# A fused convolution, mixture and upsampling kernel: a ring of three residual buffers (five at the end), and bilinear upsampling split by axis

## The chip, the cores and the metric

The kernel runs on one core of one Trainium2 chip. The metric is the device time of one execution in microseconds. All inputs and the output lie in device memory; x and the output are 268 MB each.

## The reference

x is a float32 tensor of 8 batches, 512 channels, 128 x 128. What is computed (cut to what matters):

```python
# block 1, with sx = x
x = conv(sx, w_down, stride 2, pad 1, groups=256)        # 2 channels -> 1, 3x3: (8, 256, 64, 64)
labels = kmeans(normalised x[0])                         # 8 clusters of the 256 channels, 10 iterations
v5 = mean of x over the channels of each cluster         # (8, 8, 64, 64)
mu, var = gmm_fit(v5 as 4096 points of 8 numbers)        # 2 components, 10 EM iterations, for each batch
gate = sigmoid(sum over components of ordered mu * w_conv)[:, cluster of the channel]
pre_up = gate * x + x
up = repeat(pre_up, 2, axis=1) * w_up                    # (8, 512, 64, 64)
y = bilinear_up_x2(up) + sx                              # (8, 512, 128, 128)
def bilinear_up_x2(x):
    rows = x[:, :, y0, :] * (1 - fy) + x[:, :, y1, :] * fy
    return rows[:, :, :, x0] * (1 - fx) + rows[:, :, :, x1] * fx
# block 2, on y (weights w_guide, w_fuse, bn_*)
s = clip(w_guide @ mean of y over the image, 0, 6)       # 128 numbers per batch
shift = clip(batchnorm(w_fuse @ s), 0, 6)                # 512 numbers per batch
out = y + shift
```

So for each batch: out = x + shift + scale * (bilinear upsampling of the small convolution result), where scale and shift are numbers per channel that are known only once the whole batch has been convolved and its EM iterations have run. x is therefore read twice: once for the convolution, once as the residual.

## The kernel before

**Tiling.** A batch is 16 steps (`STEPS`): two tiles `t` of 128 small channels, by eight blocks of 16 image rows (`S` = 8, counted by `u` from 0 to 3 and `h` 0 or 1). A step convolves 16 rows of 256 input channels to 8 rows of 64 for 128 channels, and upsamples 8 rows of 64 to 16 rows of 128, each used for the two output channels that share it.

**Stages.** Stage `j` (0 to 9) convolves batch j, runs EM of batch j-1 and writes out batch j-2, step by step side by side. Stage 0 only convolves; then comes the clustering; stage 1 convolves and runs EM; stages 2 to 7 do all three; stage 8 (`B`) does EM and output; stage 9 only output. In a stage with EM the first two steps are "start" (means and variances), ten are "iterate" (an EM iteration each), and the last four "finish" (the gate, and the two small layers behind `scale` and `shift`, L797 and L805, which stand once in each such stage, at t = 1, u = 2, h = 1 and the step behind it).

**Engines and queues, for one step** with all three parts:

- *SP* moves the residual. `stage_body` (L389 to L413) waits for `result[i]`, stores both channels of the step (L398), then waits until those two stores have landed (L404) and reloads the same buffers for the step two further on (L380). The residual tile `xres` has one buffer for each h, so two steps' worth. In the last two stages (L442 to L450) the two buffers of `xin`, free by then, join it as spares, and the reload runs three steps ahead.
- *ACT*, in order: copies the transposed pairs from PSUM to `pairs` (L580, L583); the logarithms of EM (L588); sums of the input for the mean (L592); the exponentials of EM (L599); adds `shift` to the residual in place once it has landed (L611); copies the convolution out of PSUM (L617); issues the load of `xin` for two steps on (L625, L351), 2048 KB.
- *PE*, in order: the transposes of `stage`, one (L817) into the bank of the convolution and eight (L824) into two banks; the convolution, 18 matmuls of 64 output columns that alternate between the halves of the array (L679; each float32 matmul is two instructions); in the last eight steps of a stage the cluster means (L690); the EM sums (L835, L861); the upsampling, nine matmuls (L877) of `pairs` by `interp`.
- *POOL*: copies the small rows needed to `stage` (L503, L505); the halo row of `xin` (L470); the EM coefficients (L483 to L487); and once the upsampling of the step before is done, the product of row weights and column weights `interp` (L512), 16 x 128 numbers, anew for each step.
- *DVE*: EM expectation, sums and update; then `xres = up * scale + xres` (L1235), six instructions for the step, three for each channel.

A pair is two neighbouring small rows of 64 for all 128 channels, transposed, so that the 128 partitions are (row, column) and one matmul applies both axes of the bilinear weights. `runs` (L289) decides whether a stage's steps are written out or looped; DVE and ACT loop over the stages 2 to 7, and over the steps in them. In PSUM, bank 0 is shared by the convolution and the transpose of L817, and banks 3 to 6 hold the 16 upsampled rows.

## Time and profile before

| | |
|---|---|
| median of 3 runs | 2568.73 us (2557.87 to 2576.21) |
| the profiled execution | 2567.7 us, span 2565.9 us |
| mean granted TensorE clock | 0.888 |
| busy of the span: PE, DVE, ACT, POOL | 85%, 49%, 51%, 27% |
| moved by DMA | 808.43 MB, mean 315 GB/s |
| of it SP's queue and ACT's queue | 542.34 MB and 264.25 MB |
| idle of ACT ahead of L611, most of it for reloads of xres | 411.1 us |
| idle of PE ahead of L877, most of it for POOL's L512 | 120.7 us |

Busy times and waits are of one profiled execution. Idle time of an engine matters only where the engine is on the path that sets the end; the chain of work that ended last is followed back from the last instruction, at each step to what released it. Two lines of the profile's page cut the span into 40 equal slices and show how full the DMA engines are and what they move:

```
DMA  6631144699999999999999999899989999877999
GB/s 248 240 120 66 66 174 166 240 359 352 351 356 351 343 362 359 356 348 346 362 376 338 344 345 361 339 347 348 344 334 358 350 358 361 345 293 285 383 425 402
```

The first eight slices are stages 0 and 1 with the clustering between them; the slices from the ninth on have the output in them, the last six or so only the output.

### The profile page before, as it was taken

The page shows a single profiled execution, that of the slowest core. Times are in us where ns is not written, and L with a number is a line of the kernel's source. Part 1 is how long each engine was busy: PE and PEld are TensorE (multiplying, and loading weights), DVE is VectorE, ACT ScalarE, POOL GpSimd, SP SyncE. Part 2 cuts the span into 40 slices and gives each one's busy share as a digit, 9 for nine tenths or more (in the row PEclk, how much of TensorE's full clock was granted, in tenths as well). Part 3 has the DMA queues.
Part 4 walks back from the last instruction along what each step waited for, and adds up shares of the span by engine and source line. Part 5 has one row for each costly group of instructions (what it writes and reads, how often), then busy time and mean ns, then how long its engine had stood idle before and what let it go on. Part 6 is the DMA issues. An engine that isn't in the chain of part 4 may idle for free.

```text
span 2565.9 us, 35348 instructions
## 1 busy us (share of the span) xinstructions
PE 2189.4 (85%) x10521; PEld 1300.6 (51%) x10521; DVE 1263.0 (49%) x3232; ACT 1310.4 (51%) x1710; POOL 705.5 (27%) x841
## 2 busy tenths in 40 slices
PE   8995699998999899988998899888998899655764
PEld 2355634554554556544564455445554455544653
DVE  0054343265535554465535554455535654677654
ACT  5531044565555555565555555555555555434554
POOL 0000011232323322332333322332322322333453
PEclk9995598999999888999899889998999989877887
DMA  6631144699999999999999999899989999877999
GB/s 248 240 120 66 66 174 166 240 359 352 351 356 351 343 362 359 356 348 346 362 376 338 344 345 361 339 347 348 344 334 358 350 358 361 345 293 285 383 425 402
DMA packets 109839, 808.43 MB, mean 315 GB/s; under 512 B 10880, under 2 KB 10880, under 8 KB 11392
## 3 DMA queue, kind: packets, MB, share of 16 engines
q1 hardware_dynamic: 75424, 542.34, 54.4%
q10 hardware_dynamic: 34272, 264.25, 27.5%
q8 instruction: 81, 1.33, 0.2%
q14 instruction: 62, 0.51, 0.1%
HBM read 538.12 MB, written 268.44 MB: 314 GB/s over the span
## 4 chain that ended last, share of the span: by engine, by line
PE 51%; DMA 31%; issue 5%; DVE 5%; POOL 2%; DVEq 2%; ACTq 1%; POOLq 1%; SPq 1%; ACT 0%
PE ps L679 26%; DMA out<-xres 21%; PE ps L877 12%; DMA xres<-x 6%; PE ps L690 4%; DMA xin<-x 3%; PE ps L824 2%; POOL interp L512 2%; PE ps L835 2%; DVE xres L1235 1%; DMA out<-xin 1%; PE ps L735 1%; ACTq L620 1%; DVEq L1239 1%; POOLq L504 1%
## 5 line engine op out<-in xcount | busy, mean ns | idle before, releaser
L679 PE MATMUL ps<-xin,taps 128*64 128x512 f32 (+1 forms) x4608 | 1100.1, 631 | 16.0 <-DMA xin<-x 13.8
L1235 DVE SCALAR_TENSOR_TENSOR xres<-ps,scale,xres 128x1024 f32<-128x1024 f32 (+2 forms) x672 | 591.9, 924 | 310.6 <-PE ps L877 249.4
L877 PE MATMUL ps<-interp,pairs 128*128 128x256 f32 (+1 forms) x2304 | 611.9, 432 | 120.7 <-POOL interp L512 91.0
L679 PEld LDWEIGHTS ps<-xin,taps 128*64 128x64 f32 x4608 | 336.3, 139 | 696.4 <-issue 684.0
L611 ACT ACTIVATE xres<-xres,shift 128x2048 f32<-128x2048 f32 x224 | 444.9, 1998 | 411.1 <-DMA xres<-x 408.6
L512 POOL TENSOR_TENSOR interp<-cst 128x2048 f32<-128x2048 f32 x128 | 462.2, 3611 | 661.3 <-PE ps L877 659.2
L877 PEld LDWEIGHTS ps<-interp,pairs 128*128 128x128 f32 x2304 | 505.6, 233 | 212.9 <-issue 64.8
L592 ACT ACTIVATE junk<-xin 128x2048 bf16<-128x2048 f32 x256 | 489.3, 1911 | 35.9 <-issue 25.8
L483 POOL TENSOR_TENSOR coef<-mu,ivar 128x16 f32<-128x16 f32 x80 | 17.7, 221 | 906.0 <-DVEq L923 906.0
L580 ACT ACTIVATE pairs<-ps 128x128 f32<-128x128 f32 x128 | 35.2, 275 | 311.1 <-PE ps L817 310.9
L583 ACT ACTIVATE pairs<-ps 128x512 f32<-128x512 f32 x256 | 140.1, 596 | 13.2 <-PE ps L824 10.3
L824 PE MATMUL ps<-cst,stage 128*128 128x128 f32 x1024 | 143.3, 287 | 0.0
L690 PEld LDWEIGHTS ps<-mean_w,conv 128*128 128x128 f32 x896 | 104.3, 192 | 46.9 <-issue 46.9
L617 ACT ACTIVATE conv<-ps 128x512 f32 (+1 forms) x128 | 74.5, 582 | 101.2 <-PE ps L679 101.0
L824 PEld LDWEIGHTS ps<-cst,stage 128*128 128x128 f32 x1024 | 124.6, 148 | 0.0
L817 PE MATMUL ps<-cst,stage 128*128 128x128 f32 x128 | 38.6, 302 | 93.3 <-ACTq L620 87.8
L905 DVE TENSOR_TENSOR blk<-ps,cst 128x16 f32<-128x16 f32 x80 | 13.9, 174 | 195.0 <-PE ps L835 195.0
L690 PE MATMUL ps<-mean_w,conv 128*128 128x8 f32 x896 | 109.2, 258 | 0.0
L470 POOL COPY xin<-xin 128x256 f32<-128x256 f32 x112 | 62.6, 559 | 166.5 <-PE ps L679 120.9
L1235 DVE SCALAR_TENSOR_TENSOR xin<-ps,scale,xin 128x1024 f32<-128x1024 f32 (+2 forms) x96 | 83.6, 923 | 40.3 <-ACT xin L611 26.2
L599 ACT ACTIVATE resp<-logp 128x32 f32<-128x32 f32 x160 | 27.9, 221 | 147.5 <-DVEq L1108 143.4
L835 PEld LDWEIGHTS ps<-resp,feat 128*128 128x128 f32 x640 | 78.8, 194 | 44.3 <-issue 25.6
(170 smaller groups left out, 1416.5 us busy)
## 6 DMA issues: line engine op xcount, KB each, us to landing
xin<-x ACTq DMA_DIRECT2D x126, 2048.0 KB, 14.9
xres<-x SPq DMA_DIRECT2D x224, 1024.0 KB, 10.3
out<-xres SPq DMA_DIRECT2D x224, 1024.0 KB, 13.9
xin<-x SPq DMA_DIRECT2D x32, 1024.0 KB, 14.1
out<-xin SPq DMA_DIRECT2D x32, 1024.0 KB, 11.0
xin<-x SPq DMA_DIRECT2D x2, 2048.0 KB, 11.9
cst<-consts SPq DMA_DIRECT2D x1, 412.0 KB, 3.0
wg<-w_guide SPq DMA_DIRECT2D x1, 256.0 KB, 12.9
```

Source lines behind the costliest of these rows:

```text
L470: pool.tensor_copy(xin[:, h, :, 0, :], xin[:, 1 - h, :, XR, :]).then_inc(halo, 1)
L512: pool.tensor_tensor(interp[:, :, :], cst[:, ds(C_COEF + XR * (2 * u + h), XR)].unsqueeze(2).to_broadcast([P, XR, W]), cst[:, C_U:C_U + W] ...
L583: act.activation(pairs[:, 4 * i:4 * i + 4, :].rearrange("c r w -> c (r w)"), ps[:, PS_T + i, :], ACT.Copy).then_inc(tc[1 + i], 1)
L592: act.activation(junk[:, :], xin[:, h, i, 1:, :].rearrange("c r w -> c (r w)"), ACT.Copy, accum_out=xsum[:, p, t, i, ds(2 * u + h, 1)])
L611: act.activation(c, c, ACT.Identity, bias=shift[:, p, 2 * t + i:2 * t + i + 1]) \
L617: act.activation(conv[:, p, ds(t * PX + CN * (2 * u + h), CN)], conv_sum(do_out, h).rearrange("c r w -> c (r w)"), ACT.Copy, accum_out=csu ...
L679: mm = pe.matmul(half[:, :, 1:] if kx == 0 else half, taps[:, 2 * t + i, n, :], tap_input(h, i, ky, kx), start=n == 0, stop=n == len(TAPS) ...
L690: m = pe.matmul(ps[:, bank, c * K:(c + 1) * K], conv[:, p, t * PX + c * P:t * PX + (c + 1) * P], weights[:, t, :], start=t == 0, stop=t == ...
L824: mm = pe.transpose(ps[:, PS_T + i, m * P:(m + 1) * P], stage[:, k:k + 2, :].rearrange("c r w -> c (r w)"), ident)
L835: m = pe.matmul(ps[:, PS_SMALL, SM_BLK:SM_BLK + N * GC] .rearrange("p (n c) -> p n c", n=N), feat[:, GC * q:GC * (q + 1), :].rearrange("p ...
L877: mm = pe.matmul(ps[:, PS_UP + pos // 4, (pos % 4) * W:(pos % 4 + n) * W], pairs[:, m, :], interp[:, pos:pos + n, :].rearrange("c r w -> c ...
L1235: m = dve.scalar_tensor_tensor(dst, up[:, pos * W:(pos + r1 - r0) * W], sc, dst, ALU.mult, ALU.add)
```

## The change

The residual tile `xres` gets three buffers (`SLOTS`), used in turn by output step `o` (0 to 127); from step 96 (`FULL`, the first of stage 8) on the two buffers of `xin` join them, five in all. SP runs one written-out loop over all output steps: it stores step o, then reloads the step two ahead (four ahead in the last two stages), into the buffer whose store was issued a step before. Because the turn of three does not fit loops of two, the stages with output are written out on SP, ACT and DVE.

The upsampling is split by axis. POOL now makes the 16 upsampled rows, still 64 wide, itself: differences of neighbouring small rows (`rise`), times the fraction of each output row (`step_`), plus the upper small row (`new`, in `lines`); `above` keeps the last small row for the next step. It waits for the EM responsibilities of the iteration before (`em_resp`) ahead of the sums. PE transposes pairs of those rows (eight transposes, none in the bank of the convolution) and applies the column weights alone, straight from the constants, with 64 rows of the array for each output row: 16 matmuls of 128 columns, the even row of a pair on the lower partitions into one bank, the odd row on the upper ones into another. DVE scales and adds in eight instructions, every second row of the output each. The product `interp` and its wait are gone.

The diff, cut (of SP's part only what is new is shown; what it replaces is in the listing above):

```diff
--- before.py
+++ after.py
+SLOTS = 3
...
         low = CR * s + (r + 1) // 2 - 1
-        pos = C_COEF + XR * s + (r - 1) % XR
-        wts = {int(y0[y]): np.float32(1) - fy[y], int(y0[y]) + 1: fy[y]}
-        assert all(row in (low, low + 1) or not v for row, v in wts.items())
-        c[:WC, pos] = wts.get(low, 0)
-        c[WC:, pos] = wts.get(low + 1, 0)
+        upper = {int(y0[y]) - 1: np.float32(1), int(y0[y]): fy[y]}
+        assert low in upper or (int(y0[y]) == low + 1 and not fy[y])
+        c[:, C_FY + LINES * s + r + 1] = upper.get(low, 1)
...
-        xres = sb("xres", [P, 2, 2, XR, W])
-        interp = sb("interp", [P, XR, W])
-        pairs = sb("pairs", [P, CR + 1, P])
-        stage = sb("stage", [P, CR + 2, WC])
+        xres = sb("xres", [P, SLOTS, 2, XR, W])
+        pairs = sb("pairs", [P, CR, P])
+        lines = sb("lines", [P, 2, LINES, WC])
+        rise = sb("rise", [P, CR + 1, WC])
...
-        def residual(j, t, u, h, i):
-
-            if isinstance(j, int) and j >= B:
-                uses = U * (j - B) + U // 2 * t + u // 2
-                if u % 2:
-                    return xin[:, h, i, 1:, :], spare_in[h][i], 16 * uses + 16, spare_stored[h][i]
-                return xres[:, h, i, :, :], xres_in[h][i], 8 * STEPS * (B - 2) + 16 * uses + 16, stored[h][i]
-            return xres[:, h, i, :, :], xres_in[h][i], 8 * (STEPS * (j - 2) + S * t) + 16 * u + 16, stored[h][i]
+        FULL = STEPS * (B - 2)
+
+        def residual(o, i):
+
+            n = o - FULL
+            if n < 0:
+                q, use = o % SLOTS, o // SLOTS
+            else:
+                q, use = n % (SLOTS + 2), n // (SLOTS + 2)
+                if q >= SLOTS:
+                    h = q - SLOTS
+                    return xin[:, h, i, 1:, :], spare_in[h][i], 16 * use + 16, spare_stored[h][i]
+                use += FULL // SLOTS
+            return xres[:, q, i, :, :], xres_in[q][i], 16 * use + 16, stored[q][i]
 
...
+            def reload(o):
                 for i in range(2):
+                    tile, landed, count, freed = residual(o, i)
+                    if count > 16:
                         sp.wait_ge(freed, count - 16)
                     sp.dma_start(tile.rearrange("c r w -> c (r w)"),
+                                 dram_channel(xv, o // STEPS, o % STEPS // S, o % S, i)).then_inc(landed, 16)
+
+            def store(o):
                 for i in range(2):
+                    tile, landed, count, freed = residual(o, i)
+                    sp.wait_ge(result[i], o + 1)
+                    sp.dma_start(dram_channel(ov, o // STEPS, o % STEPS // S, o % S, i),
                                  tile.rearrange("c r w -> c (r w)")).then_inc(freed, 16)
+
+            END = B * STEPS
+            sp.wait_ge(km_done, 1)
+            for o in range(SLOTS):
+                reload(o)
+            for o in range(END):
+                if o == FULL:
+                    sp.wait_ge(conv_ps, B * STEPS)
+                    sp.wait_ge(xsummed, B * STEPS)
+                    sp.wait_ge(halo, B * STEPS)
+                    reload(o + SLOTS)
+                    reload(o + SLOTS + 1)
+                store(o)
+                ahead = SLOTS - 1 if o <= FULL else SLOTS + 1
+                if o > 0 and o + ahead < END:
+                    reload(o + ahead)
+            for o in range(END - SLOTS - 2, END):
                 for i in range(2):
+                    tile, landed, count, freed = residual(o, i)
+                    sp.wait_ge(freed, count)
 
...
-                def rows(t, u, h):
+                def sums_taken(n):
+                    return EM_ITERS * (j - 1) + n if do_em else EM_ITERS * B
+
+                def upsample_rows(t, u, h, top, sums):
+
                     o = STEPS * (j - 2) + S * t + 2 * u + h
-                    wait_all(pool,
-                             (tp[2], o + 1))
-                    pool.tensor_copy(stage[:, 0, :], stage[:, CR, :])
+                    here = conv[:, p, ds(t * PX + CN * (2 * u + h), CN + WC)] \
+                        .rearrange("c (r w) -> c r w", w=WC)
+                    new, step_ = (lines[:, q, :, :].rearrange("c (k v) w -> c k v w", v=2) for q in range(2))
+                    part_ = cst[:, ds(C_FY + LINES * (2 * u + h), LINES)].rearrange("c (k v) -> c k v", v=2)
+                    if top and h == 0:
+                        pool.memset(above[:, :], 0.0)
+                        pool.drain()
+                    pool.tensor_tensor(rise[:, 0, :], here[:, 0, :], above[:, :], ALU.subtract)
+                    pool.tensor_tensor(rise[:, 1:, :], here[:, 1:, :], here[:, 0:CR, :], ALU.subtract)
                     pool.drain()
-                    pool.tensor_copy(stage[:, 1:, :],
-                                     conv[:, p, ds(t * PX + CN * (2 * u + h), CN + WC)]
-                                     .rearrange("c (r w) -> c r w", w=WC)).then_inc(staged, 1)
-
-                def weights(t, u, h):
-                    o = STEPS * (j - 2) + S * t + 2 * u + h
-                    pool.wait_ge(up_ps[1], o + 1)
-                    pool.tensor_tensor(
-                        interp[:, :, :],
-                        cst[:, ds(C_COEF + XR * (2 * u + h), XR)].unsqueeze(2).to_broadcast([P, XR, W]),
-                        cst[:, C_U:C_U + W].unsqueeze(1).to_broadcast([P, XR, W]),
-                        ALU.mult).then_inc(interp_ready, 1)
+                    pool.tensor_tensor(step_, rise[:, :, :].unsqueeze(2).to_broadcast([P, CR + 1, 2, WC]),
+                                       part_.unsqueeze(3).to_broadcast([P, CR + 1, 2, WC]), ALU.mult)
+                    pool.drain()
+                    wait_all(pool, (em_resp, sums), (tp[1], o + 1))
+                    pool.tensor_tensor(new[:, 0, 1, :], step_[:, 0, 1, :], above[:, :], ALU.add)
+                    pool.tensor_tensor(new[:, 1:, :, :], step_[:, 1:, :, :],
+                                       here[:, 0:CR, :].unsqueeze(2).to_broadcast([P, CR, 2, WC]), ALU.add)
+                    pool.drain()
+                    pool.tensor_copy(above[:, :], here[:, CR - 1, :])
+                    pool.drain().then_inc(staged, 1)
 
                 def round_(t, u, top, em=None):
                     for h in range(2):
                         if do_out:
-                            rows(t, u, h)
+                            before = EM_ITERS if t == 1 else 0
+                            upsample_rows(t, u, h, top, sums_taken(em + h if em is not None else before))
                         if do_conv:
                             halo_of(t, u, h, top)
                         if em is not None:
                             em_coefficients(EM_ITERS * (j - 1) + em + h, (EM_ITERS + 1) * (j - 1) + em + h)
-                        if do_out:
-                            weights(t, u, h)
 
                 if do_out:
-                    pool.wait_ge(conv_done, STEPS * (j - 1))
+                    wait_all(pool, (conv_done, STEPS * (j - 1)))
...
-                        act.wait_ge(tp[0], o + 2)
-                        act.activation(pairs[:, CR, :], ps[:, PS_CONV, 0:P], ACT.Copy).then_inc(tc[0], 1)
                         for i in range(2):
-                            act.wait_ge(tp[1 + i], o + 2)
+                            act.wait_ge(tp[i], o + 2)
                             act.activation(pairs[:, 4 * i:4 * i + 4, :].rearrange("c r w -> c (r w)"),
-                                           ps[:, PS_T + i, :], ACT.Copy).then_inc(tc[1 + i], 1)
+                                           ps[:, PS_T + i, :], ACT.Copy).then_inc(tc[i], 1)
...
-                runs(do_em, act, round_, not do_conv, True)
+                runs(do_em, act, round_, do_out, True)
...
-            with act.Fori(1, B // 2 - 1) as jj:
-                for p in range(2):
-                    stage_body(2 * jj + p, p, True, True, True)
-            for p in range(2):
-                stage_body(B - 2 + p, p, True, True, True)
+            for j in range(2, B):
+                stage_body(j, j % 2, True, True, True)
...
-                if do_out:
-                    pe.wait_ge(tc[0], o + 2)
...
-                        pe.wait_ge(conv_taken, g + 2 if do_conv else B * STEPS + 2)
-                        pe.transpose(ps[:, PS_CONV, 0:P],
-                                     stage[:, CR:CR + 2, :].rearrange("c r w -> c (r w)"), ident) \
-                            .then_inc(tp[0], 1)
                         for i in range(2):
-                            pe.wait_ge(tc[1 + i], o + 1)
+                            pe.wait_ge(tc[i], o + 1)
                             for m in range(4):
-                                k = 4 * i + m
+                                k = CR * i + 2 * m + 1
                                 mm = pe.transpose(ps[:, PS_T + i, m * P:(m + 1) * P],
-                                                  stage[:, k:k + 2, :].rearrange("c r w -> c (r w)"), ident)
-                            mm.then_inc(tp[1 + i], 1)
+                                                  lines[:, 0, k:k + 2, :].rearrange("c r w -> c (r w)"), ident)
+                            mm.then_inc(tp[i], 1)
...
-                        pe.wait_ge(interp_ready, o + 1)
-                        for i in range(3):
-                            pe.wait_ge(tc[i], o + 2)
-
-                        for half, ms in ((0, (1, 2, 3, 4)), (1, (5, 6, 7, 8, 0))):
+                        for half in range(2):
+                            pe.wait_ge(tc[half], o + 2)
                             pe.wait_ge(up_taken[half], o + 1)
-                            for m in ms:
-                                pos, n = (2 * m - 2, 2) if 0 < m < CR else (2 * CR - 2, 1) if m else (2 * CR - 1, 1)
-                                mm = pe.matmul(ps[:, PS_UP + pos // 4, (pos % 4) * W:(pos % 4 + n) * W],
-                                               pairs[:, m, :],
-                                               interp[:, pos:pos + n, :].rearrange("c r w -> c (r w)"),
-                                               start=True, stop=True)
+                            for m in range(4):
+                                for odd, at in enumerate((slice(0, WC), slice(WC, P))):
+                                    mm = pe.matmul(ps[:, PS_UP + 2 * half + odd, m * W:(m + 1) * W],
+                                                   pairs[at, 4 * half + m, :], cst[at, C_U:C_U + W],
+                                                   start=True, stop=True)
                             mm.then_inc(up_ps[half], 1)
...
-                                up = ps[:, PS_UP:PS_UP + 4, :].rearrange("c b n -> c (b n)")
-                                spans = [(1, 9, 0)] if half == 0 else [(9, XR, CR), (0, 1, XR - 1)]
-                                for r0, r1, pos in spans:
-                                    dst = residual(j, t, u, h, i)[0][:, r0:r1, :].rearrange("c r w -> c (r w)")
-                                    m = dve.scalar_tensor_tensor(dst, up[:, pos * W:(pos + r1 - r0) * W],
-                                                                 sc, dst, ALU.mult, ALU.add)
+                                for odd in range(2):
+                                    up = ps[:, PS_UP + 2 * half + odd, :].rearrange("c (m w) -> c m w", w=W)
+                                    dst = residual(o, i)[0][:, CR * half + odd:CR * (half + 1):2, :]
...
-                runs(do_em, dve, round_, not do_conv)
+                runs(do_em, dve, round_, do_out)
```

## Rows read from the trace of the kernel before

**Rows 1.** The page, chain that ended last: shares of the span by line.

```profile
PE ps L679 26%; DMA out<-xres 21%; PE ps L877 12%; DMA xres<-x 6%; PE ps L690 4%; DMA xin<-x 3%; PE ps L824 2%; POOL interp L512 2%; PE ps L835 2%; DVE xres L1235 1%; DMA out<-xin 1%; PE ps L735 1%; ACTq L620 1%; DVEq L1239 1%; POOLq L504 1%
```

**Rows 2.** The same chain in order of time: start, length in us, what.

```profile
773.90 15.41 DMA out<-xres
789.53 12.01 DMA xres<-x
```

**Rows 3.** Windows: length, busy us of PE, PEld, DVE, ACT, POOL; PEclk, DMA share, GB/s.

```profile
780.00:1040.00 260.00, 239.23 (x1136) 139.20 (x1133) 133.96 (x346) 143.74 (x188) 78.08 (x96) 0.89 0.92 353
1280.00:1300.00 20.00, 20.00 (x99) 12.77 (x97) 5.46 (x7) 9.87 (x12) 4.81 (x4) 0.83 0.99 399
2440.00:2566.00 126.00, 69.14 (x315) 58.24 (x315) 63.51 (x74) 60.13 (x57) 49.55 (x34) 0.82 0.98 413
```

**Rows 4.** The page, DMA issues: queue, count, KB each, median us to landing.

```profile
xin<-x ACTq DMA_DIRECT2D x126, 2048.0 KB, 14.9
xres<-x SPq DMA_DIRECT2D x224, 1024.0 KB, 10.3
out<-xres SPq DMA_DIRECT2D x224, 1024.0 KB, 13.9
```

**Rows 5.** Line L797, stages 2 and 7: ns min/median/max, first and last start us.

```profile
L797 PE MATMUL ps<-chmean,wgx x8: 249/251/251, 709.7 to 710.5; 128*128 128x1 f32 x8
...
L797 PE MATMUL ps<-chmean,wgx x8: 250/251/251, 2149.9 to 2150.7; 128*128 128x1 f32 x8
```

**Rows 6.** Timeline of one step with EM: start, us, engine, line, what, idle before.

```profile
823.07 0.39 ACTq L351 DMA_DIRECT2D xin<-x  x1
...
824.28 8.38 PE L679 MATMUL ps<-xin,taps 128*64 128x512 f32 x36 [0.36 <-ACT pairs L580]
...
832.60 1.07 PE L835 MATMUL ps<-resp,feat 128*128 128x16 f32 x8
...
834.71 5.40 PE L877 MATMUL ps<-interp,pairs 128*128 128x256 f32 x18
...
841.01 0.33 PE L817 MATMUL ps<-cst,stage 128*128 128x128 f32 x1 [0.90 <-ACTq L620]
...
842.21 8.33 PE L679 MATMUL ps<-xin,taps 128*64 128x512 f32 x36
```

**Rows 7.** PE's groups by form, 560 to 2180 us: busy us, mean ns, idle before.

```profile
L679 PE MATMUL ps<-xin,taps 128*64 128x512 f32 x2170 | 570.9, 632 | 1.7 <-ACT pairs L580 0.9
L877 PE MATMUL ps<-interp,pairs 128*128 128x256 f32 x1260 | 382.2, 469 | 0.0
...
L877 PE MATMUL ps<-interp,pairs 128*128 128x128 f32 x360 | 54.7, 275 | 0.0
```

**Rows 8.** The page, groups: the product on POOL, and tiny operations of POOL and DVE.

```profile
L512 POOL TENSOR_TENSOR interp<-cst 128x2048 f32<-128x2048 f32 x128 | 462.2, 3611 | 661.3 <-PE ps L877 659.2
...
L483 POOL TENSOR_TENSOR coef<-mu,ivar 128x16 f32<-128x16 f32 x80 | 17.7, 221 | 906.0 <-DVEq L923 906.0
...
L905 DVE TENSOR_TENSOR blk<-ps,cst 128x16 f32<-128x16 f32 x80 | 13.9, 174 | 195.0 <-PE ps L835 195.0
```

**Rows 9.** Timeline: POOL's halo copy in two steps, the second beside VectorE's product.

```profile
827.61 0.40 POOL L470 COPY xin<-xin 128x256 f32<-128x256 f32 x1
...
844.49 1.04 DVE L905 TENSOR_TENSOR prod<-feat,cdiff 128x512 f32<-128x512 f32 x1 [0.21 <-issue]
...
844.93 0.86 POOL L470 COPY xin<-xin 128x256 f32<-128x256 f32 x1
```

**Rows 10.** Timeline of one EM step of stage 8 (no convolution).

```profile
2268.79 5.32 DVE L1235 SCALAR_TENSOR_TENSOR xres<-ps,scale,xres 128x1024 f32<-128x1024 f32 x6 [0.19 <-issue]
...
2273.65 6.41 PE L877 MATMUL ps<-interp,pairs 128*128 128x256 f32 x18 [5.70 <-POOL interp L512]
...
2279.89 0.96 PE L835 MATMUL ps<-resp,feat 128*128 128x16 f32 x8
...
2283.93 5.32 DVE L1235 SCALAR_TENSOR_TENSOR xin<-ps,scale,xin 128x1024 f32<-128x1024 f32 x6 [0.20 <-issue]
```

84 lines of the change are left out of this document (15 added, 69 removed).

## The prediction

> **What bounds the kernel now.** I read first the chain that ended last, by line [rows 1]: after the convolution's matmuls (L679, 26%) come 21% of stores out of the residual tile and 6% of reloads into it. In order of time [rows 2] one such pair reads store 15.41 us, reload 12.01 us, each from issue to landing: a reload of a buffer may not be issued before that buffer's store has landed, and with two buffers this round trip lies on the path once in two steps. Together with two ACT passes and the vector engine's part it makes about 36 us per two steps.
>
> Second, the windows [rows 3]. Over 260 us in mid-kernel PE is busy 239 us at a mean granted clock of 0.89 (most of it at the 2.4 GHz level, the rest at 1.2), the DMA engines are 92% busy and move 353 GB/s. So three candidates stand close together: the two-buffer round trip, PE, and transfers. In 20 us of an EM-free stretch PE is busy for all of them, and DMA runs at 0.99 and 399 GB/s. The last 126 us move 413 GB/s at 0.98.
>
> Third, the price of a step. It moves 2048 KB (xin) and four times 1024 KB (two reloads, two stores) [rows 4], 6144 KB or 6.29 MB. The excite matmuls of L797 stand once in each stage, at the same step [rows 5]: 709.7 to 2149.9 us are five stages of 16 steps, 288.0 us each, 18.0 us a step.
>
> The time to beat is that of the profiled execution, 2567.7 us (span 2565.9, 1.8 around it); the median of the runs is 2568.7, so no correction is made.
>
> **The ring.** Reload of step o+2 used to be issued after the store of step o had landed; now it waits for the store of o-1, issued a whole step earlier. On SP's queue the order is store(o), then reload(o+2): what stands behind that new wait is store(o+1), whose result is a step away, so the wait holds nobody unless a store takes over a step to land (median 13.9 us, [rows 4], against 18.0). That takes the 15 us store out of the chain. Next in line are:
>
> - *DMA.* 353 GB/s at 92% is 384 GB/s when never idle: 6.29 MB / 384 = 16.4 us a step. From the 399 GB/s at 0.99 of the short stretch it would be 15.6 us.
> - *PE.* One EM step at full clock [rows 6]: convolution from 824.28, 8.38 us; block sums at 832.60; upsampling at 834.71, 5.40 us; nine transposes 841.01 to the next convolution at 842.21. In between PE waited 0.90 us for ACT's copy of the convolution, which stood behind a residual that came late; that goes too.
> - *xin loads.* ACT issues one at 823.07 [rows 6], 16.7 us after the start of one convolution, for the next but one, at 842.21: 19.1 us. At a period of 16.5 that is 2 x 16.5 - 16.7 = 16.3 us if ACT is no earlier in its step than now (it should be, as it waits less for residuals), against a median landing of 14.9 us [rows 4]. Covered, with 1.4 us to spare at the least.
>
> **The upsampling on PE.** Nine matmuls with 128 rows (seven of 256 columns, two of 128; each is two instructions) become 16 with 64 rows and 128 columns, 32 instructions, alternating between the upper and the lower half of the array and between two banks. Columns stay 2048. Prices [rows 7]: an instruction of 128 columns takes 54.7/360 = 152 ns of PE time, one of 256 columns 382.2/1260 = 303. Without any overlap of the halves the new form costs 32 x 152 = 4.9 us, no gain over 5.40 worth the name. With overlap: the convolution's matmuls already use the halves of the other axis, and each lasts 632 ns while 36 of them finish in 8.38 us, one per 233 ns [rows 6, 7], so halves do run together there. By that, half of 4.9, 2.4 us, and I take 2.6. The Trainium skill, TensorEngine Tiling (Array Packing), Key Properties, says that row tiles work in parallel but that changing the tiling mode drains the array; no run here prices a change into row tiles, and by its first half alone the term is the 2.4. One transpose fewer saves about 0.1 us. PE's step becomes 8.4 + 1.1 + 1.0 + 2.6 + 1.1, 14.2 to 14.5 us at full clock and about 15.7 at 0.9, below 16.4. So this half of the change is worth little by itself; it keeps PE from becoming the bound once the ring is gone.
>
> **POOL.** The interpolation product goes: 3611 ns [rows 8], started only after the upsampling of the step before. In come two differences (64 and 512 elements), a product (1152), two sums (64 and 1024), and a copy. From 3611 ns for 2048 elements and 221 for 16 the slope is 1.67 ns: 2816 x 1.67 + 5 x 0.19 + copy 0.24 + four drains of 0.12, about 6.4 us. Old copies and product together were 4.5. It is ahead of the transposes now, so I check its cover. The part behind the wait for em_resp is sums and copy, 2.8 us. In the EM step of [rows 6] the responsibilities are there by 832.60, so the rows would be staged by 835.4, and PE wants them at 834.71 + 2.6 = 837.3. Margin 1.9 us. If VectorE work slows it (the halo copy takes 0.40 us alone and 0.86 beside the 512-element product, [rows 9]), 2.2 us of sums become 4.7 and the margin is -0.6 us. Bounds for a step: 0 and +0.6; I take 0, since behind em_resp VectorE has only tiny operations for 3 us. EM coefficients wait behind the sums on POOL, but their reader, the next expectation, comes after 5 us of VectorE work.
>
> **VectorE and ACT.** Eight instead of six scale-and-add instructions: 2 x 0.17 us at the price of a tiny one [rows 8], on an engine 52% busy. Output rows at a stride of two: bounds 0 and a doubling of 5.3 us; I take 0, the elements are runs of 128. ACT loses one copy and its wait. The EM loop through these engines is seen in the drain stages [rows 10]: 2268.79 to 2283.93, 15.1 us. It held 5.70 us of PE waiting for POOL's product, which put block sums at 2279.89, so at most 1 us of it goes and 0.35 comes back: 14.5 to 14.8. Also below 16.4. ACT, DVE and SP run straight code instead of loops; no row prices its fetching, bounds -0.2 and +0.5 us a step (PE already runs such code inside its loop), taken as 0.
>
> **Sum.** DMA sets the step: 16.4 us, plus 1% of idle, 16.5 (the bounds: 15.6 and 17.2). Five stages: 80 x (18.0 - 16.5) = 120 us. The 13 steps before the first mark: 0 to 20, I take 5, as they are partly quicker already. Three steps after the last mark: 4.5. Ten EM steps of the drain at 0.5: 5. Last stage: its transfers are at 0.98 [rows 3], one more buffer prefetched is worth at most half a step: 5. Stages 0, 1 and the clustering: untouched, 0. In all 139.5: 2567.7 - 139.5 = **2428 us**.
>
> **Rivals.**
>
> *A. Traffic is already at its rate.* No more than 353 GB/s in the mix of two reads to one write; the busy share rises to 1.00 and packets only stretch. Then a step takes 6.29/353 = 17.8 us, 80 x 0.2 + 10 = 26 us: 2542. For it: long mid-kernel stretches stay at it. Against: 399 GB/s for 20 us [rows 3]. The Trainium skill, DMA: Bandwidth & Descriptors, Specifications, gives an HBM limit of about 358 GB/s per core, which speaks against this change; by it a step would be 17.6 and the estimate about 2520. The last stage's 413 is above it, with as many stores as loads. Chance 0.12, half of it under 1%.
>
> *B. Another loop takes over at 17.2 us:* the EM loop lengthened by POOL contention, or xin landings past 16.3 us. 80 x 0.8 + 15 = 79: 2489. Chance 0.14.
>
> *C. Slower: half-height matmuls do not pipeline.* If each is spaced by its whole latency, some 275 ns (those of 128 columns now), the upsampling costs 8.8 us and PE's step 17.9 - 0.9 + 3.4 = 20.4. It decides from 6.3 us on (195 ns an instruction). 80 x 2.4 = 192 slower, less 10 in the drain: 2750. Against: overlap of column halves. Chance 0.06.
>
> *D. The rate goes to that of the short stretch,* 15.6 us a step: 80 x 2.4 + 25 = 217: 2351. Chance 0.08.
>
> **Numbers.** Forecast 0.60 (its own range, 16.2 to 17.0 a step: 2404 to 2472). Range 2375 to 2525: all of the forecast and B, the lower part of A. Left out: D, C, most of A. Under 1% (26 us) a change of this kernel could hardly be told from none. Faster by over 1%: 0.60 + 0.14 + 0.08 + 0.05 = 0.87; within: 0.07; slower: 0.06.
>
> **What would show it.** Ring: stores of the residual nearly gone from the chain, ACT's wait for reloads (the largest of its waits) near zero, marks of L797 264 us apart, 375 to 385 GB/s at 0.97 or more. Upsampling: 32 instructions in 2.4 to 2.9 us. POOL: PE does not wait for it, nearly 6.4 us busy a step. Wrong if the share is at 1.00 with the rate under 360 (A), if PE waits for staged rows or xin (B), or if the 32 take over 6 us (C).

## The result, and the profile after

The changed kernel takes 2357.6 us (median of 4 runs, 2354.2 to 2361.4) against 2570.7 of before: ratio 0.918, 95% interval 0.914 to 0.922. That is 8.2% faster, outside the forecast range (2375 to 2525) and next to the 2351 us of rival D, which was given 0.08.

The marks of the excite matmuls (now L767) show where the time went. The columns are those of [rows 5]:

```profile
L767 PE MATMUL ps<-chmean,wgx x8: 250/250/251, 694.1 to 694.9; 128*128 128x1 f32 x8
...
L767 PE MATMUL ps<-chmean,wgx x8: 249/250/251, 1936.6 to 1937.4; 128*128 128x1 f32 x8
```

Five stages take 1242.5 us, 248.5 each and 15.53 us a step, against 288.0 and 18.0: 197.7 us gained. Up to the first mark 15.6 us are gained (694.1 for 709.7). From the last mark to the end nothing is: 2352.4 - 1936.6 = 415.8 us, before 416.0. The sum, 213.5, is the difference of the spans (2565.9 and 2352.4).

The windows of the changed kernel, for comparison with [rows 3]:

```profile
780.00:1040.00 260.00, 237.17 (x1538) 132.81 (x1540) 166.82 (x411) 163.35 (x200) 125.02 (x163) 0.93 1.00 410
1280.00:1300.00 20.00, 17.45 (x116) 10.01 (x114) 15.96 (x38) 13.44 (x20) 10.71 (x18) 0.91 1.01 426
2226.00:2352.00 126.00, 57.55 (x437) 52.03 (x434) 63.41 (x94) 55.15 (x45) 65.37 (x61) 0.63 0.99 418
```

The third number from the end is the granted clock, then the share of the DMA engines, then GB/s. The share rose from 0.92 to 1.00, and the rate by more than that, from 353 to 410. So a busy engine also moves more: 16 engines x 8192 bytes x share / rate is the mean time that an engine takes for 8192 bytes, the size of a full packet, 342 ns before and 320 ns now. That is the number the forecast had held fixed. It is called the time of a packet below.

The chain that ended last, by line, for [rows 1] (L649 is the convolution, L839 the upsampling, L789 the transposes, L800 the block sums):

```profile
PE ps L649 34%; PE ps L839 8%; PE ps L660 6%; DVE xres L1195 5%; PE ps L789 4%; DMA xres<-x 4%; PE ps L800 3%; DMA out<-xres 3%; DVEq L1198 2%; DMA xin<-x 2%; DVE part L866 2%; DMA out<-xin 2%; PE ps L826 1%; PE ps L705 1%; DVE xin L1195 1%
```

Stores fell from 21% to 3%. SP's queue stood 1204.7 us for stores of the residual before and 71.9 us now, and ACT 408.6 us for its reloads before and 115.3 us now. New on the chain is `DVE part L866`, VectorE's tiny product of EM. Between 700 and 1936 us, the five stages of the marks, the chain holds 5% of residual loads and 1% of loads of `xin`; the convolution has 39% of it, the upsampling 12%, and through the EM steps it runs from PE to VectorE and back. One EM step, for [rows 6] (start, us, what):

```profile
782.14 5.57 DVE L1195 SCALAR_TENSOR_TENSOR xres<-ps,scale,xres 128x512 f32<-128x512 f32 x8 [0.19 <-issue]
...
783.99 8.33 PE L649 MATMUL ps<-xin,taps 128*64 128x512 f32 x36 [0.70 <-ACTq L595]
...
792.26 1.06 PE L800 MATMUL ps<-resp,feat 128*128 128x16 f32 x8
...
792.74 2.34 POOL L490 TENSOR_TENSOR lines<-lines,conv 128x1024 f32<-128x1024 f32 x1
...
793.85 1.28 DVE L866 TENSOR_TENSOR part<-cst,bsum 128x32 f32<-128x32 f32 x1
...
795.21 0.41 PE L826 MATMUL ps<-part,ones 128*128 128x34 f32 x2 [1.89 <-DVEq L867]
...
797.48 5.57 DVE L1195 SCALAR_TENSOR_TENSOR xres<-ps,scale,xres 128x512 f32<-128x512 f32 x8 [0.19 <-issue]
...
810.90 2.06 PE L839 MATMUL ps<-cst,pairs 64*128 64x128 f32 x32
```

The step is 797.48 - 782.14 = 15.34 us (EM steps of 16.1 and 14.5 us alternate, and this is their mean). The upsampling's 32 instructions take 2.06 us. And VectorE's product `part`, 194 ns before, starts at 793.85 and ends at 795.13, when POOL's sum of 1024 elements has just ended (792.74 + 2.34 = 795.08).

### The profile page after: what moved, and what is told of

Read it like the earlier page. It is cut to its first block, busy times and chain, and to the rows that moved or that the text cites. A ratio compares the mean times of both kernels' runs of the same rounds, so it can differ in the third digit from the quotient of the medians.

```text
span 2352.4 us, 37758 instructions
## 1 busy us (share of the span) xinstructions
PE 1974.8 (84%) x12185; PEld 1163.7 (49%) x12185; DVE 1345.7 (57%) x3488; ACT 1276.0 (54%) x1582; POOL 961.8 (41%) x1240
## 4 chain that ended last, share of the span: by engine, by line
PE 61%; DVE 18%; DMA 12%; DVEq 4%; issue 3%; ACT 1%; ACTq 0%; SPq 0%
PE ps L649 34%; PE ps L839 8%; PE ps L660 6%; DVE xres L1195 5%; PE ps L789 4%; DMA xres<-x 4%; PE ps L800 3%; DMA out<-xres 3%; DVEq L1198 2%; DMA xin<-x 2%; DVE part L866 2%; DMA out<-xin 2%; PE ps L826 1%; PE ps L705 1%; DVE xin L1195 1%
## 5 line engine op out<-in xcount | busy, mean ns | idle before, releaser
L649 PE MATMUL ps<-xin,taps 128*64 128x512 f32 (+1 forms) x4608 | 1082.9, 623 | 18.2 <-DMA xin<-x 14.6
L1195 DVE SCALAR_TENSOR_TENSOR xres<-ps,scale,xres 128x512 f32<-128x512 f32 x928 | 634.0, 745 | 131.3 <-PE ps L839 66.6
L649 PEld LDWEIGHTS ps<-xin,taps 128*64 128x64 f32 x4608 | 335.9, 137 | 683.2 <-issue 676.3
L586 ACT ACTIVATE xres<-xres,shift 128x2048 f32<-128x2048 f32 x232 | 455.5, 1993 | 118.3 <-DMA xres<-x 115.3
L839 PE MATMUL ps<-cst,pairs 64*128 64x128 f32 x4096 | 367.4, 348 | 107.6 <-DVE xres L1195 68.2
L839 PEld LDWEIGHTS ps<-cst,pairs 64*128 64x128 f32 x4096 | 335.6, 252 | 120.8 <-issue 115.9
L489 POOL TENSOR_TENSOR lines<-lines,above 128x64 f32<-128x64 f32 x128 | 41.0, 320 | 642.9 <-DVEq L1078 374.3
L490 POOL TENSOR_TENSOR lines<-lines,conv 128x1024 f32<-128x1024 f32 x128 | 303.5, 2371 | 0.0
L485 POOL TENSOR_TENSOR lines<-rise,cst 128x1152 f32<-128x1152 f32 x128 | 271.3, 2120 | 23.8 <-issue 13.2
L789 PE MATMUL ps<-cst,lines 128*128 128x128 f32 x1024 | 192.2, 349 | 21.4 <-POOLq L494 11.0
L789 PEld LDWEIGHTS ps<-cst,lines 128*128 128x128 f32 x1024 | 155.3, 182 | 42.5 <-issue 24.3
L483 POOL TENSOR_TENSOR rise<-conv 128x512 f32<-128x512 f32 (+1 forms) x128 | 164.1, 1282 | 0.1
L592 ACT ACTIVATE conv<-ps 128x512 f32<-128x512 f32 (+1 forms) x128 | 74.4, 581 | 102.5 <-PE ps L649 102.3
L826 PE MATMUL ps<-part,ones 128*128 128x34 f32 x160 | 36.9, 316 | 104.6 <-DVEq L867 104.6
L800 PEld LDWEIGHTS ps<-resp,feat 128*128 128x128 f32 x640 | 81.0, 199 | 76.5 <-DVEq L1078 68.8
```

What stands on the lines that cost most here:

```text
L483: pool.tensor_tensor(rise[:, 1:, :], here[:, 1:, :], here[:, 0:CR, :], ALU.subtract)
L485: pool.tensor_tensor(step_, rise[:, :, :].unsqueeze(2).to_broadcast([P, CR + 1, 2, WC]), part_.unsqueeze(3).to_broadcast([P, CR + 1, 2, WC ...
L490: pool.tensor_tensor(new[:, 1:, :, :], step_[:, 1:, :, :], here[:, 0:CR, :].unsqueeze(2).to_broadcast([P, CR, 2, WC]), ALU.add)
L586: act.activation(c, c, ACT.Identity, bias=shift[:, p, 2 * t + i:2 * t + i + 1]) \
L649: mm = pe.matmul(half[:, :, 1:] if kx == 0 else half, taps[:, 2 * t + i, n, :], tap_input(h, i, ky, kx), start=n == 0, stop=n == len(TAPS) ...
L789: mm = pe.transpose(ps[:, PS_T + i, m * P:(m + 1) * P], lines[:, 0, k:k + 2, :].rearrange("c r w -> c (r w)"), ident)
```

## The experiments

Theory Q: SP's queue used to run empty, since SP stood waiting for a store to land before it issued anything else; a packet takes longer where its queue starts or runs dry, and this is what held the rate at 353 GB/s. Its rival, theory C: the old upsampling's own traffic in SBUF stretched the packets.

**The ring alone.** The old upsampling with the new ring:

```diff
-        xres = sb("xres", [P, 2, 2, XR, W])
+        xres = sb("xres", [P, SLOTS, 2, XR, W])
...
(SP's block, residual() and the written-out loops of ACT and DVE as in the change;
 PE, POOL, interp, stage and pairs as before)
```

> The ring of three (five) residual buffers and the written-out loops, with the old upsampling (product on POOL, nine full-height matmuls). Theory Q (transfers slow down only where a queue runs empty; the ring keeps SP's queue filled): the stretched packets go also here, 8192-byte packets of mid-kernel average under 330 ns against 343 before, and the DMA share falls, since PE is then the bound: 8.4 + 1.1 + 1.0 + 5.4 + 1.2 = 17.1 us a step at full clock, some 17.4 with the clock at 0.92. Time about 2500 to 2530. Theory C (the old upsampling's own SBUF traffic stretched the packets, and the split cured it): DMA share stays near 0.95 to 1.00 at 350 to 385 GB/s, time 2440 to 2530 with DMA full. Theory R (the ring alone brings nearly all): 2360 to 2400.

2426.8 us, ratio to before 0.945 (0.940 to 0.950). Both are of three runs; a fourth took 7060 us, and nothing on record says why.

```profile
780.00:1040.00 260.00, 248.96 (x1253) 142.42 (x1251) 146.74 (x357) 157.67 (x205) 88.68 (x100) 0.94 0.95 383
```

PE is busy 249 of 260 us and is the bound, as theory Q had it; its marks are 263.0 us apart, 16.44 us a step, one microsecond below the expected 17.4, because 5.4 us was not the upsampling's time at full clock (below). The upsampling takes 3.71 or 5.40 us an EM step, as before, and yet a packet takes 16 x 8192 x 0.95 / 383 = 325 ns. The time lies in none of the three ranges given ahead, and share and rate would fit C's words too; what speaks against C is the packet time, which it has at 342 ns here, and, more plainly, the transfers alone below.

**The split alone,** with two buffers and the old wait:

```diff
-SLOTS = 3
+SLOTS = 2
...
-                ahead = SLOTS - 1 if o <= FULL else SLOTS + 1
-                if o > 0 and o + ahead < END:
+                ahead = SLOTS if o < FULL else SLOTS + 1
+                if o != FULL and o + ahead < END:
```

> The upsampling split by axis with two residual buffers (four in the last two stages), a reload issued only after the store of the same buffer has landed, as before. Theory Q and the chain of the kernel before: store and reload still take turns, some 28 us and 8 us of ACT and DVE for two steps, so 17.5 to 18.0 us a step, packets around 340 ns, time 2520 to 2570. Theory C: packets average 315 ns, transfers land sooner, 16.5 us a step or less, time under 2450.

2542.8 us, ratio 0.990 (0.986 to 0.994). PE has become idle and it hardly helps: 221 of 260 us busy, 359 GB/s, a packet 347 ns, 36% of the chain are stores, and SP stands 1506 us for them. Theory C wanted under 2450 us here.

```profile
780.00:1040.00 260.00, 220.76 (x1370) 116.68 (x1368) 147.49 (x382) 146.74 (x180) 113.35 (x148) 0.89 0.95 359
```

So 1.0% for the split, 5.5% for the ring, 8.2% for both: they are worth 1.7 points more together, since the ring hands the bound to PE and the split takes it from there.

**Transfers alone.** All computation left out (the comments in this cut are added); ACT reloads `xin` as soon as a load has landed, SP loads the residual and stores it unchanged. First with two buffers and the wait for the store of the same buffer:

```diff
+            for o in range(END):
+                store(o)                  # waits until the load of o has landed
+                if DEPTH <= o + 2 < END:
+                    reload(o + 2)         # waits for the buffer's last store
```

> No computation at all: only the loads of xin (two buffers, each reloaded when the last has landed), the loads of the residual into two buffers, and its stores unchanged (x goes to the output); a reload waits for the store of its own buffer. All 128 steps run the mix of two loads to one store. Theory Q: SP's queue runs empty in each turn; packets average 330 ns or more; 16.0 us a step or more, 2050 us in all or more. Theory C: nothing computes, so packets stand at 310 ns and the engines are full: 14.9 us a step, 1910 us.

2144.1 us (one run). Then the same with three buffers (`DEPTH` 3):

> The same transfers without computation, with three residual buffers: the reload for the step two further on waits for the store issued one step earlier. Theory Q: SP's queue never runs empty, packets 309 to 315 ns, 420 to 427 GB/s, 14.8 to 15.0 us a step, 1900 to 1920 us in all. A limit of device memory near 358 GB/s for this mix would give 17.6 us a step and 2250 us. Theory C: as with two buffers.

1902.7 us (one run), 14.86 us a step. Two windows of each, two buffers first; columns after the length are POOL, clock, share, GB/s:

```profile
400.00:1000.00 600.00, 0.00 (x0) 1.00 1.01 425
1400.00:2000.00 600.00, 0.00 (x0) 1.00 0.86 307
```

```profile
400.00:1000.00 600.00, 0.00 (x0) 1.00 1.01 426
1400.00:1800.00 400.00, 0.00 (x0) 1.00 1.01 427
```

In the first window of each, ACT's loads (which nothing paces here) run beside SP's and fill the engines, and 425 GB/s are moved even with two buffers, three bytes read for each one written. Later they are done and SP's queue is alone, one byte read for each one written: 307 GB/s with two buffers and 427 with three. So the queue's filling sets the rate, with nothing computing. Theory Q is shown here for SP's queue by itself; beside it the kernel has ACT's, paced by the computation, which no run without computation has.

The records of the single packets say where the time goes. In the second window the median of the full packets of SP's queue is 309 ns in either run, but with two buffers their mean is 368. The first that follow an empty queue take some 800 ns, and 309 after 1.5 us; where the reload gives way to the stores, with nothing queued behind, they take about 500 for some 4 us. The last ahead of an empty queue take 309. With three buffers the mean is 309 as well.

The kernel's own mix, two bytes read for each one written, is that of the whole run: 424 GB/s on average with three buffers. The Trainium skill, DMA: Bandwidth & Descriptors, Specifications, has a limit of about 358 GB/s a core for device memory, half of what it gives a memory stack that two cores share. Here one core runs, and it is not held to that. The measurement decides.

**Three buffers, the old wait.** The edit is that of the split alone, second part, with `SLOTS` 3:

> The changed kernel with its three (five) buffers, but each reload waits for the store of the same step, as with two buffers, and goes three steps ahead. Latency theory (the third buffer helps because the round trip is off the path): the reload still has two steps to land, nothing waits for it, time 2350 to 2370. Queue theory (it helps because SP's queue never runs empty): with this wait nothing is queued behind the store, which lands 7 to 10 us after its issue, and then only the reload is queued; packets of SP's queue go from 314 to some 330 ns, the rate from 410 to 385 to 395 GB/s, a step from 15.5 to 16.0 to 16.4 us, time 2390 to 2430.

2507.0 us, ratio 0.975 (0.969 to 0.980). The direction is theory Q's, the size is two to four times what it gave (149 us over the changed kernel, for 32 to 72). The chain in order of time shows why, stores without a reload between them:

```profile
894.86 15.26 DMA out<-xres
911.24 18.25 DMA out<-xres
930.45 17.52 DMA out<-xres
948.93 16.00 DMA out<-xres
964.95 14.11 DMA xres<-x
```

And SP's queue of the same kernel:

```profile
787.10 0.93 SPq L404 DMA_DIRECT2D out<-xres  x2
801.78 2.80 SPq L397 DMA_DIRECT2D xres<-x  x2
804.62 1.67 SPq L404 DMA_DIRECT2D out<-xres  x2
819.77 0.34 SPq L397 DMA_DIRECT2D xres<-x  x1
```

SP issues the stores, stands for 14.7 us until they have landed, issues the reloads (2.8 us), and only then comes to the next stores: 804.62 - 787.10 = 17.5 us. That is a loop of its own, once a step, through one engine's order of issue; the next six turns on this queue take 16.1 to 18.6 us. How many buffers there are hardly enters into it: the marks are 17.3 us a step apart here and 17.5 in the split alone, with two.

**Two buffers, the new place of the wait.** `SLOTS` 2 in the changed kernel, nothing else:

> The changed kernel with two residual buffers in the stages with convolution, but with the new place of the wait: the reload of step o+1 follows the store of o and waits for the store of o-1. SP is then never held for a store's landing, yet a reload has only one step to land: landing 10 to 13 us, ACT 4 us, VectorE 5.6 us after it are in line, 20 to 23 us a step. If the place of the wait alone were the gain, time 2360 to 2420. If both are needed, slower than the kernel before: 2700 to 3000.

2869.6 us, ratio 1.114 (1.110 to 1.119). The wait is in the right place and the buffer for it is missing: ACT waits 1003 us for reloads. So both are needed, and the third buffer is what pays for moving the wait.

**The order of the half-height matmuls.**

```diff
-                            for m in range(4):
-                                for odd, at in enumerate((slice(0, WC), slice(WC, P))):
+                            for odd, at in enumerate((slice(0, WC), slice(WC, P))):
+                                for m in range(4):
```

> The changed kernel with the upsampling matmuls in another order: in each bank pair first the four on the lower half of the array, then the four on the upper, instead of in turn. If the halves run together only when their instructions alternate, the 32 take 3.6 to 4.9 us instead of 2.06. PE has 1 to 2 us to spare in an EM step, so the time moves by 0 to 40 us: 2355 to 2400. If the short form is cheap for another reason, they stay at 2.1 us and the time at 2357.

2546.6 us, ratio 0.990 (0.986 to 0.994): nearly all of the change's gain is lost by the order of sixteen matmuls, far more than the 0 to 40 us expected. Three of its PE rows, one upsampling at full clock, and the windows of two of its upsamplings (columns as in [rows 3]):

```profile
788.40 2.82 PE L839 MATMUL ps<-cst,pairs 64*128 64x128 f32 x32
...
800.43 1.06 PE L800 MATMUL ps<-resp,feat 128*128 128x16 f32 x8
...
803.30 0.64 PE L826 MATMUL ps<-part,ones 128*128 128x34 f32 x2 [1.81 <-DVEq L867]
...
803.87 5.13 PE L839 MATMUL ps<-cst,pairs 64*128 64x128 f32 x32
```

```profile
788.50:791.10 2.60, 2.60 (x32) 2.52 (x32) 1.65 (x9) 0.06 (x1) 1.08 (x5) 1.00 1.02 432
804.00:809.00 5.00, 5.00 (x33) 4.78 (x34) 2.60 (x9) 0.00 (x0) 2.55 (x7) 0.50 1.01 426
```

At the 2.4 GHz level (clock 1.00) the 32 instructions take 2.82 us for the 2.06 of the alternating order. That is 37% more and short of the 3.6 to 4.9 us expected, so the groups of four still overlap in part. At the 1.2 GHz level (0.50) they take 5.13. Most steps fall between, 4.0 to 4.4 us, since the lower level now comes in nearly every step at this place; in the changed kernel it comes in about half, for 2.6 to 3.8 us. Over 260 us the granted clock is 0.84 against 0.93, and PE is the bound again, busy for 248 us. Shown is that the order costs 0.76 us at equal clock, and that the rest came with the lower clock. Why this order draws the lower level was not settled. The Trainium skill, TensorEngine Tiling (Array Packing), Key Properties, has the halves working in parallel; the trace agrees, and adds that the order of the instructions decides how far.

**Where POOL's sums stand.** Without the wait in each step:

```diff
-                    return EM_ITERS * (j - 1) + n if do_em else EM_ITERS * B
+                    return EM_ITERS * (j - 1) if do_em else EM_ITERS * B
```

> The changed kernel without the wait for the responsibilities in each step (only that of the stage before is waited for), so POOL's sums start as soon as PE has read the rows of the step before. If the collision with VectorE is what the EM loop pays, the sums now meet the expectation's 512-element product (0.69 us alone) and 4 us of small operations: EM steps grow by 1 to 2 us, time 2380 to 2450. If the place of the sums doesn't matter, 2350 to 2365.

2409.0 us, ratio 0.937 (0.933 to 0.941). The collision moved to the expectation: its product takes 1825 ns in place of 693, the small product behind it (`lsum`) 744 in place of 178, and `part` is back at 194:

```profile
L866 DVE TENSOR_TENSOR prod<-feat,cdiff 128x512 f32<-128x512 f32 x57 | 104.0, 1825 | 7.8
...
L866 DVE TENSOR_TENSOR part<-cst,bsum 128x32 f32<-128x32 f32 x57 | 11.1, 194 | 4.9 <-issue 0.8
```

**Most of the sums left out:**

```diff
-                    pool.tensor_tensor(new[:, 1:, :, :], step_[:, 1:, :, :],
-                                       here[:, 0:CR, :].unsqueeze(2).to_broadcast([P, CR, 2, WC]), ALU.add)
+                    pool.tensor_tensor(new[:, 1:2, :, :], step_[:, 1:2, :, :],
+                                       here[:, 0:1, :].unsqueeze(2).to_broadcast([P, 1, 2, WC]), ALU.add)
```

> The changed kernel whose POOL sum of 1024 elements is cut to 128, so that most upsampled rows are left out (wrong rows go through the rest). It takes 2.1 us off POOL and the collision off VectorE (its tiny product beside that sum took 1.28 and 0.47 us instead of 0.19). If the EM loop over PE, DVE and POOL sets the step (15.34 us in the timeline), it falls by 0.3 to 1.1 us and the time by 30 to 60 us, to 2300 to 2325. If transfers set the step, nothing moves: 2350 to 2362.

2314.3 us, ratio 0.900 (0.897 to 0.904). So with the DMA share at 0.99 to 1.00 the EM loop still had a part in the step.

**The product as operations with a scalar,** which is the first attempt to get this for nothing:

```diff
-                tt(part[:, :, 0:2 * K], cst[:, C_MF:C_MF + 2 * K].unsqueeze(1).to_broadcast([P, N, 2 * K]),
-                   bsum[:, :].unsqueeze(2).to_broadcast([P, N, 2 * K]), ALU.mult).then_inc(em_part, 1)
+                for n in range(N):
+                    dve.tensor_scalar(part[:, n, 0:2 * K], cst[:, C_MF:C_MF + 2 * K], bsum[:, n:n + 1],
+                                      None, ALU.mult)
+                dve.drain().then_inc(em_part, 1)
```

> The changed kernel with VectorE's small product of two tensors (128x32, which takes 0.19 us alone and up to 1.28 us beside POOL's sums) made of two multiplications by a scalar per partition, 16 elements each, the same values. If POOL's sums hold up only operations with two tensor inputs, these take 2 x 0.17 us and the EM step falls by 0.2 to 0.9 us: time 2315 to 2345, up to the 2314 of the shortened sums. If they are held up as well, nothing is gained: 2350 to 2365.

2365.0 us, ratio 0.921 (0.916 to 0.925): no gain. These are held as well, two of 503 ns on average:

```profile
L1085 DVE TENSOR_SCALAR part<-cst,bsum 128x16 f32<-128x16 f32 x114 | 52.4, 503 | 4.8 <-issue 0.4
```

**The sums in four pieces, and in two** (there with 4 for each 2 in these lines):

```diff
-                    pool.tensor_tensor(new[:, 1:, :, :], step_[:, 1:, :, :],
-                                       here[:, 0:CR, :].unsqueeze(2).to_broadcast([P, CR, 2, WC]), ALU.add)
+                    for a in range(0, CR, 2):
+                        pool.tensor_tensor(new[:, a + 1:a + 3, :, :], step_[:, a + 1:a + 3, :, :],
+                                           here[:, a:a + 2, :].unsqueeze(2).to_broadcast([P, 2, 2, WC]), ALU.add)
```

> The changed kernel with POOL's sum of 1024 elements issued as four of 256, the same values. If VectorE's product of two tensors is held until the running POOL instruction ends (both times seen it ended with it), it now waits for at most 256 elements, 0.6 us, and mostly less: the EM step gains 0.3 to 0.8 us, POOL pays 0.5 us more. Time 2310 to 2345. If it is held for the whole run of POOL's instructions, or merely slowed, nothing is gained: 2355 to 2370.

> The same with two of 512. The product of VectorE falls near the end of the first: 2320 to 2355, between the changed kernel and the four, if a running instruction is what holds it; 2355 to 2365 if not.

2326.5 us in four pieces, ratio 0.904 (0.901 to 0.907); 2328.2 us in two, 0.904 (0.901 to 0.908). Both beat the changed kernel's 0.918 with intervals apart, with the same arithmetic. The product's mean goes from 722 to 352 ns (changed kernel first, then four pieces; in two it is 400). Were it held through the whole row of POOL's instructions, or only slowed beside them, the pieces would have gained nothing:

```profile
L866 DVE TENSOR_TENSOR part<-cst,bsum 128x32 f32<-128x32 f32 x58 | 41.9, 722 | 5.0 <-issue 0.8
```

```profile
L867 DVE TENSOR_TENSOR part<-cst,bsum 128x32 f32<-128x32 f32 x57 | 20.1, 352 | 4.9 <-issue 0.8
```

70 EM steps of stages 2 to 8 at 0.37 us are 26 us of the 31 gained, if all of it lay on the path; between the marks of stages 2 and 7 the gain is 17.4 us, for 50 such steps. This is the fastest version run.

## Why the prediction was wrong

**The step that failed is the DMA term,** "353 GB/s at 92% is 384 GB/s when never idle: 16.4 us a step". It took the time of a packet as fixed and only the idle share as what the ring could fill. The runs show 410 GB/s at 1.00 in the changed kernel and 427 without computation: 14.7 to 15.3 us for 6.29 MB. Rates above 384 were visible in [rows 3]: 399 GB/s at 0.99, and 413 at 0.98 in the last stage. They were kept for a bound and a rival with 0.08. The choice of the long window over the short one was the wrong one: a share averaged over a stretch whose queue keeps running dry also averages in the slow packets of a queue that has just started or has little behind it. At 15.53 for 16.5 us a step, 80 steps make 78 us. The steps before the first mark gave 15.6 us for 5, and what follows the last mark 0.2 for 14.5, so 2428 missed by 74 (by 70 against the median of the runs).

With it fell "DMA sets the step". Transfers have only about 6% of the chain of the five stages, so most of the 15.53 us is PE's matmuls and the small operations between them. PE's own term, "about 15.7 at 0.9", was the closer one, partly by luck: it had 2.6 us for the upsampling's 2.06 and nothing for the cluster means, 1.95 us in the last eight steps of each stage. Nor is rival D's mechanism shown by its number: at 410 to 427 GB/s transfers by themselves would take less than its 15.6 us.

**The chain.** That the store would leave it was right, its form was not. The text had a round trip of 36 us through two buffers once in two steps. Three buffers under the old wait show a loop of SP alone, store issued, landed, reload issued, next store, 17.5 us in each step. [rows 2] had the start of it, and the pieces behind those rows go on the same way, four stores on end:

```profile
827.14 15.90 DMA out<-xres
...
845.02 16.22 DMA out<-xres
...
863.32 17.45 DMA out<-xres
...
882.35 15.61 DMA out<-xres
...
898.17 13.98 DMA xres<-x
```

The remedy was the same by either reading, so this cost no accuracy, but only the second says which half of the change matters.

**The upsampling.** 2.4 to 2.6 us expected, 2.06 at full clock measured. Rival C (275 ns an instruction) is out. But its old price was misread: [rows 6] were called a step at full clock, and their 5.40 us were not. Two neighbouring steps before, and a window inside the 5.40 us:

```profile
797.64 3.71 PE L877 MATMUL ps<-interp,pairs 128*128 128x256 f32 x18
...
834.71 5.40 PE L877 MATMUL ps<-interp,pairs 128*128 128x256 f32 x18
```

```profile
834.80:840.00 5.20, 5.20 (x19) 4.22 (x18) 2.50 (x8) 1.66 (x2) 0.84 (x4) 0.67 1.01 424
```

The clock there is 0.67; at the upper level the old form takes 3.71 us. So the split saves 1.65 us of PE at equal clock and not 2.8. That the split is worth little by itself was right (1.0%). So was that it keeps PE from becoming the bound once the store's wait is gone: the ring alone stops at 2427 us with PE busy for 249 of 260, and the split takes 69 us more off.

**POOL.** Its operations in a step are 0.32 + 1.28 + 2.12 + 0.32 + 2.37 + 0.24 = 6.65 us, 6.4 expected. The 6.4 had 0.48 of drains in it, so the operations cost 0.7 us more than thought. The collision was put on the wrong side. The text asked whether VectorE would slow POOL and took 0, as VectorE has only tiny operations there; it was POOL's long instruction that held one of those until it ended, 0.5 us a step on average. The EM loop was expected at 14.5 to 14.8 us and is 15.34. PE hardly waits for the staged rows (11 us in the whole run), as forecast.

**VectorE.** Eight instructions take 5.57 us, 5.66 expected, and the stride costs nothing. No run singles out the written-out loops, and no wait in the trace points to them.

**Smaller slips.** The load of `xin` at 823.07 stands 17.0 us after the start of a convolution (806.07) and not 16.7, so the cover was 1.1 us and not 1.4. The upper end of the forecast's own range, 17.0 us a step, gives 2468 and not 2472. ACT's wait for reloads was to be near zero and is 115 us. None of these moved the forecast.

**The drain.** 14.5 us were expected from the last mark on and 0.2 came. The EM steps of stage 8, for [rows 10]:

```profile
2099.71 5.57 DVE L1195 SCALAR_TENSOR_TENSOR xin<-ps,scale,xin 128x512 f32<-128x512 f32 x8 [0.19 <-issue]
...
2111.75 0.90 DVE L866 TENSOR_TENSOR part<-cst,bsum 128x32 f32<-128x32 f32 x1 [0.40 <-issue]
...
2112.74 0.64 PE L826 MATMUL ps<-part,ones 128*128 128x34 f32 x2 [1.85 <-DVEq L867]
...
2115.22 5.57 DVE L1195 SCALAR_TENSOR_TENSOR xin<-ps,scale,xin 128x512 f32<-128x512 f32 x8 [0.19 <-issue]
```

15.51 us against 15.14: the wait for the old product went, the held `part`, a quarter of a microsecond more in VectorE's scale-and-add and a lower clock came. Around it the granted clock is 0.56, against 0.73 at the same place before, and the matmuls of L826 last 0.64 us for 0.41. PE was given more of the lower level (1.2 GHz) just where it sits in a chain of small operations; why is not shown.

Rival A (the rate at its limit) is refuted by the 410 to 427 GB/s. Rival B (another loop takes over) is partly true, at 15.3 and not at 17.2 us. What stays open is how 15.53 us divide between the EM loop, PE and transfers. Cutting the sums gave 1.8 points with the share still at 0.99 to 1.00, so the EM loop has a part; in four pieces, residual loads have 8% of the chain over 700 to 1936 us for the changed kernel's 5%, so transfers are next in line.

## What to carry to other kernels

When a queue's engine waits for a store to land before it issues the next transfer, that loop runs once per step, with two buffers as with three: put a whole step between a transfer and the wait for it, and give it the buffer that this takes. A DMA share below 1 is not only idle time to be filled, since packets are also slower in a queue that has just been empty or has nothing behind it; read the attainable rate from the stretch where the share is highest. And keep a long two-input instruction of POOL in pieces where VectorE is in a chain of small operations.

## What the runs showed of the hardware

- One core moved 424 GB/s over a whole run of transfers with two bytes read for each one written, 427 with one read for each written, and 410 over 260 us beside computation. SP's queue alone, with a wait for its own store in each turn, moved 307; the first packets after its empty stretches took some 800 ns, those of a filled queue 309.
- A tiny VectorE operation was held until the POOL instruction beside it ended: 194 ns alone, 1.30 us at worst beside a sum of 1024 elements, and the 512-element product 1825 ns on average for 693. The form with one tensor and a scalar per partition was held too.
- 32 matmul instructions on 64 rows and 128 columns took 2.06 us when the halves of the array alternated and 2.82 us when four of a half stood together, both at the 2.4 GHz level; with the second order the 1.2 GHz level came in nearly every step.
